# A macaron block with an SSM on one core: the gate's logits with the weights stationary in four column strips, transposed back by one instruction per group

## The reference

```python
def _L0_ffn_ref(hidden_states, gate_w, shared_gate, shared_up, shared_down, r_gate, r_up, r_down):
    ...
    shared_out = _swiglu(x, shared_gate, shared_up, shared_down)
    logits = x @ gate_w.T
    top_id = jnp.argmax(logits, axis=-1)
    score = jax.nn.sigmoid(jnp.max(logits, axis=-1))
    xs = x * score[:, None]
    ...
x = L0_attn_x
x = x + 0.5 * _L0_ffn_ref(_layernorm(x, axis=-1), ...)
x = x + _L0_attn_ref(_layernorm(x, axis=-1), ...)
x = x + 0.5 * _L0_ffn_ref(_layernorm(x, axis=-1), ...)
```

## Time and profile before

| | |
|---|---|
| median of 3 runs | 948.54 us (945.77 to 955.72) |
| the profiled execution | 946.78 us, its span 944.6 us |
| TensorE busy | 884.2 us, 94% of the span |
| TensorE weight load busy | 773.7 us, 82% |
| VectorE, ScalarE, GpSimd busy | 478.7, 383.5, 465.2 us |
| the logits matmuls, L434, TensorE busy | 33.5 us, 256 records |
| mean granted TensorE clock | 0.973 of full |

### The profile page before, as it was taken

The page is one execution under the profiler, slowest core; times in us unless marked ns, Lnnn a source line. Parts: engine busy times, 40 slices in busy tenths (PEclk is TensorE's granted clock), DMA queues, the critical chain, the costliest instruction groups (busy, mean ns, idle before and its releaser), DMA issues.

```text
span 944.6 us, 16359 instructions
## 1 busy us (share of the span) xinstructions
PE 884.2 (94%) x5422; PEld 773.7 (82%) x5423; DVE 478.7 (51%) x1008; ACT 383.5 (41%) x749; POOL 465.2 (49%) x427
## 2 busy tenths in 40 slices
PE   4999998999999999998999997999899999998998
PEld 3887787888878887887888997888788878887887
DVE  6657563333333334759898882765233323332453
ACT  3224222333333343445686763433233334333331
POOL 4424656033333305778999983576333242210883
PEclk9798999999999999998999997899999999999999
DMA  8594456246464315332011005548343555511567
GB/s 290 184 310 147 141 179 245 88 170 211 166 208 170 122 46 113 49 52 28 6 51 29 23 28 202 172 153 289 118 169 133 183 183 183 184 56 57 91 106 183
DMA packets 75292, 130.33 MB, mean 138 GB/s; under 512 B 6650, under 2 KB 67204, under 8 KB 70884
## 3 DMA queue, kind: packets, MB, share of 16 engines
q0 software_dynamic: 18688, 74.33, 25.9%
q1 hardware_dynamic: 56178, 55.21, 18.4%
q10 hardware_dynamic: 370, 0.02, 0.0%
HBM read 93.22 MB, written 36.32 MB: 137 GB/s over the span
## 4 chain that ended last, share of the span: by engine, by line
PE 73%; DMA 9%; POOL 6%; DVE 6%; issue 4%; ACT 1%; SPq 1%; ACTq 0%; POOLq 0%; DVEq 0%
PE bank L359 21%; PE bank L360 20%; PE bank L361 20%; DMA rows<-xs_sorted 8%; PE bank L426 3%; PE bank L434 3%; PE bank L559 3%; PE bank L528 2%; DVE v L1302 2%; POOL v L1535 2%; POOL hT_lo L1539 1%; POOL acc L1622 1%; DVE xT_lo L1031 1%; POOL rstd L1471 1%; POOL cbs L1497 1%
## 5 line engine op out<-in xcount | busy, mean ns | idle before, releaser
L359 PE MATMUL bank<-wr_hi,xT_hi 128*128 x312 | 130.8, 419 | 9.9 <-issue 7.6
L1596 POOL TENSOR_TENSOR wr_lo<-wr_raw,wr_hi 128x3072 fp32r<-128x3072 f32 x14 | 95.2, 6801 | 87.6 <-DMA wr_hi<-w_routed 87.6
L1622 POOL DMA_INDIRECT acc<-ys_sorted,pos x64 | 103.5, 1617 | 59.2 <-DMA ys_sorted<-rows 41.1
L361 PE MATMUL bank<-wr_lo,xT_hi 128*128 x312 | 123.9, 397 | 0.0
L360 PE MATMUL bank<-wr_hi,xT_lo 128*128 x312 | 123.9, 397 | 0.0
L1259 DVE TENSOR_TENSOR hf<-sg,bank 128x512 f32<-128x512 f32 x78 | 53.7, 689 | 136.2 <-PE bank L361 136.2
L1031 DVE TENSOR_TENSOR hT_lo<-bank,hT_hi 128x512 fp32r<-128x512 f32 x78 | 54.0, 692 | 125.3 <-ACT hT_hi L775 125.3
L359 PE MATMUL bank<-xT_hi,ws_hi 128*128 128x512 f32 x256 | 105.0, 410 | 3.9 <-DVE xT_lo L1031 3.1
L775 ACT ACTIVATE xT_hi<-bank 128x256 fp32r<-128x256 f32 (+1 forms) x126 | 56.4, 465 | 121.0 <-PE bank L528 95.7
L360 PE MATMUL bank<-xT_hi,ws_lo 128*128 128x512 f32 x256 | 103.0, 402 | 0.0
L361 PE MATMUL bank<-xT_lo,ws_hi 128*128 128x512 f32 x256 | 102.4, 400 | 0.0
(11 more groups left out here) (231 smaller groups left out, 2243.1 us busy)
## 6 DMA issues: line engine op xcount, KB each, us to landing
wr_raw<-w_routed POOLq DMA_DIRECT2D x16, 1536.0 KB, 7.1
wr_hi<-w_routed POOLq DMA_DIRECT2D x16, 1536.0 KB, 7.8
rows<-xs_sorted SPq DMA_DIRECT2D x78, 128.0 KB, 2.5
ys_sorted<-rows SPq DMA_DIRECT2D x78, 128.0 KB, 1.8
xn_kept<-xg SPq DMA_DIRECT2D x16, 512.0 KB, 3.2
rows<-xn_kept SPq DMA_DIRECT2D x16, 512.0 KB, 4.1
xg<-xn_kept SPq DMA_DIRECT2D x15, 512.0 KB, 5.0
acc<-x SPq DMA_DIRECT2D x8, 512.0 KB, 9.8
```

What stands on the lines that cost most here:

```text
L359: pe.matmul(o, a_hi, b_hi, start=start, stop=False, skip_group_check=True)
L361: return pe.matmul(o, a_hi, b_lo, start=False, stop=stop, skip_group_check=True)
L1596: pool.tensor_tensor(wr_lo[:, e % 2, :], wr_raw[:, :], f32(wr_hi[:, e % 2, :]), ALU.subtract).then_inc(s_wl, 1)
L1622: pool.indirect_dma_start(out=acc[:, tt, :], out_offset=None, in_=ys_dram, in_offset=bass.IndirectOffsetOnAxis(ap=pos[:, tt:tt + 1], axis= ...
```

## The change

The weights and the data change places. `gw_f` is padded with zeros from 8 to RG = 32 columns and is the stationary operand. The 4 tiles of a group go to 4 column strips of the array, 32 columns each, and stream 128 tokens; for each block of features the 4 strips follow each other. The result has tile t's experts on partitions 32t to 32t+7 and tokens along the free dimension. ScalarE copies this 128x128 block into `lgT` (two buffers), TensorE transposes it with one instruction (`logits_back`) into the next 128 columns of the same bank, and VectorE picks 8 of each 32 columns from there.

In the first stage the results go to other banks than the transpositions (`R1_LG`: bank 6 for groups 0 to 4, then 3, 5, 3), the transpositions no longer wait for VectorE's copy, and each transposition back stands after the next group's transpositions; the transpositions of group 6 stand before shared_down's second piece. In attention the transposition back of logits n-4 stands in iteration n between w_out and w_in.

```diff
+        R1_LG = (D2[0],) * (FB + 1) + (G2[1], U2[1], G2[1])
...
-            def logits(f, bank=LG, src=xTf):
+            def logits(f, bank=LG):
+
                 pe.wait_ge(s_xf, 2 * f + 2)
-                for t in range(GT):
-                    for kb in range(KB):
-                        mm = pe.matmul(bank[:, t * E:(t + 1) * E], src[:, kb, t * P:(t + 1) * P], gw_f[:, kb, :],
-                                       start=(t == 0 and kb == 0), stop=(kb == KB - 1), skip_group_check=True)
-                mm.then_inc(s_lg, 1)
+                for kb in range(KB):
+                    for t in range(GT):
+                        rs = slice(t * RG, (t + 1) * RG)
+                        mm = pe.matmul(bank[rs, 0:P], gw_f[:, kb, :], xTf[:, kb, t * P:(t + 1) * P], start=(kb == 0),
+                                       stop=(kb == KB - 1), skip_group_check=True, tile_position=(0, t * RG))
+                mm.then_inc(s_lq, 1)
+
+            def logits_back(f, bank=LG):
+                pe.wait_ge(s_lt, f + 1)
+                pe.transpose(bank[:, P:2 * P], lgT[:, f % 2, :], ident[:, :]).then_inc(s_lg, 1)
...
                         w_out_part(n - 2, 3)
+                    if live(n - 4):
+                        logits_back(f_ln3(n - 4))
                     if live(n):
                         w_in_part(n, 0)
...
             def r1_transposes(g):
-                if g > 0:
-                    pe.wait_ge(s_lgc, g)
                 transposes(g % 2, s_xn, g + 1, min(g, 1), f_r1(g))
...
             r1_transposes(1)
+            r1_back(0)
             pe.wait_ge(s_wsl, 1)
             shared_gu(0, 0, 0)
...
             r1_transposes(5)
+            r1_back(4)
             pe.wait_ge(s_wsl, 2)
             pe.wait_ge(s_setv, 12)
+            pe.wait_ge(s_lgc, FB + 1)
             shared_down(0, 0, 0)
             r1_logits(5)
+            r1_transposes(6)
+            r1_back(5)
             shared_down(0, 0, 1)
...
+            def logits_copy(f, bank=LG):
+                act.wait_ge(s_lq, f + 1)
+                if f >= 2:
+                    act.wait_ge(s_lg, f - 1)
+                act.activation(lgT[:, f % 2, :], bank[:, 0:P], ACT.Copy).then_inc(s_lt, 1)
...
                 for n in range(NG + 4):
                     if live(n - 1):
                         y_silu(n - 1, 2)
+                    if live(n - 4):
+                        logits_copy(f_ln3(n - 4))
                     if live(n):
                         first_tap(n, 0)
...
             def copy_logits(g, count, bank=LG):
                 dve.wait_ge(s_lg, count)
-                dve.tensor_copy(tiles(lg, g), bank[:, 0:GT * E].rearrange("p (t e) -> p t e", t=GT)).then_inc(s_lgc, 1)
+                dve.tensor_copy(tiles(lg, g), bank[:, P:2 * P].rearrange("p (t e) -> p t e", t=GT)[:, :, 0:E]).then_inc(s_lgc, 1)
```

More of the change, by code:

```diff
@@ L96, in build @@
         ones_r = sb("ones_r", [P, P], F32R)
-        gw_f = sb("gw_f", [P, KB, E], F32)
+        gw_f = sb("gw_f", [P, KB, RG], F32)
+        lgT = sb("lgT", [P, 2, P], F32)
         vec = sb("vec", [P, CB, 5], F32)
@@ L201, in build @@
         s_late = sem("small_loaded")
+        s_gwz = sem("gate_padding_cleared")
         s_x = [sem(f"x_loaded{g}") for g in range(NG)]
@@ L246, in build @@
         s_xf = sem("xTf_done")
+        s_lq = sem("logits_by_expert_done")
+        s_lt = sem("logits_by_expert_copied")
         s_lg = sem("logits_done")
@@ L719, in r1_logits, with r1_back @@
                 if g == 0:
-                    pe.wait_ge(s_xl, 2)
                     pe.wait_ge(s_late, 16 * 4)
-                logits(f_r1(g))
+                    pe.wait_ge(s_gwz, 1)
+                if 1 <= g < FB + 1:
+                    pe.wait_ge(s_lgc, g)
+                elif g == FB + 1:
+                    pe.wait_ge(s_sg, FB)
+                elif g == FB + 2:
+                    pe.wait_ge(s_h, FB)
+                elif g == FB + 3:
+                    pe.wait_ge(s_lgc, g - 1)
+                logits(f_r1(g), R1_LG[g])
+            def r1_back(g):
+                logits_back(f_r1(g), R1_LG[g])
             setup_ssm(0)
@@ L738, in _ @@
             r1_transposes(2)
+            r1_back(1)
             setup_ssm(7)
@@ L743, in _ @@
             r1_transposes(3)
+            r1_back(2)
             shared_gu(0, 0, 2)
@@ L747, in _ @@
             r1_transposes(4)
+            r1_back(3)
             shared_gu(0, 0, 3)
@@ L998, in _, with r1_copy @@
             act.activation(PQ[:, 0, :, :].rearrange("n a m -> n (a m)"), A2[:, :], ACT.Tanh).then_inc(s_seta, 1)
+            def r1_copy(g):
+                logits_copy(f_r1(g), R1_LG[g])
             xt_hi(0)
@@ L1003, in _ @@
             ws_high(1, slice(DN0, W))
+            r1_copy(0)
             xt_copy(t_r1(1))
             s_silu(0, 0, 0)
+            r1_copy(1)
             xt_copy(t_r1(2))
+            r1_copy(2)
             xt_copy(t_r1(3))
@@ L1009, in _ @@
             s_silu(0, 0, 1)
+            r1_copy(3)
             xt_copy(t_r1(4))
@@ L1013, in _ @@
             s_silu(0, 0, 3)
+            r1_copy(4)
             xt_copy(t_r1(5))
             s_hi(0, 0, 2)
+            r1_copy(5)
             xt_copy(t_r1(6))
             s_hi(0, 0, 3)
+            r1_copy(6)
             xt_copy(t_r1(7))
+            r1_copy(7)
             shared(0, 0)
@@ L1354, in _ @@
             dve.memset(GS[:, 0:1], 0.0)
+            dve.memset(gw_f[:, :, E:RG], 0.0).then_inc(s_gwz, 1)
             dve.memset(RS[:, :], 0.0)
@@ L1394, in r1_copy_logits @@
             def r1_copy_logits(g):
[L1395 removed]
+                copy_logits(g, g + 1, R1_LG[g])
             r1_stats(0)
```

10 lines of the change are left out of this document (5 added, 5 removed).

## The result

The changed kernel takes 967.88 us in the median (963.63 to 969.08), the kernel before 947.15 us beside it on the same chip (945.17 to 955.72). The ratio is 1.0195 with a 95% interval of 1.0135 to 1.0256: slower by 1.3 to 2.6%. The profiled execution took 963.63 us, its span is 961.8; the one of before took 946.78 with a span of 944.6.

A forecast was written before the change was run, and what follows sets the result against it. TensorE (PE) was taken as the bound, holding 73% of the chain. Attention's added waits, 4.5 + 2.6 + 1.6 + 0.6 + 3.0 = 12.3 us, less 0.5 in the first stage, gave +12 on 948.54: 960.5 us, range 953 to 968.

The forecast's parts named there:

- Both waits in attention: Attention: PE waits for ScalarE's lgT, then VectorE's late taps; +4.5 (n = 4, 5), +2.6, +1.6 and +0.6, +3.0 us.
- The clock: Rival: PE's new idle times bring one to three half-clock falls, up to 3 us each; 963.5 to 970.5 us; chance 0.15.
- The strips: Logits matmuls on PE: strips overlap two deep, about 0.95 us a group instead of 1.68, saving 0.75 at full clock.
- First stage: Before 72 us: PE done some 4 us earlier, mostly lost to a longer wait for the shared load; -0.5 us.
- near 71.5: First stage's end: the shared load still lands near 71.5 us, PE idling some 6 us before the first shared transpositions.
- that normalization comes out at the same time: First stage: group 6's normalization on VectorE, which the load's issue depends on, ends at the same time as before.
- the very sign that the prediction named as proof against itself: End of first stage: the shared stage starting 3 us earlier would show the forecast wrong.
- That ws_lo's subtraction would stand behind the copy of logits 0: First stage, VectorE: this subtraction, and the first gate matmuls with it, come after that copy; no separate size given.
- Strips in turn: Rival: column strips do not overlap, 1.7 us a group; waits stay, nothing saved; +18 or 966.5 us; chance 0.10.
- the waits are taken up by slack: Rival: unseen slack, mainly GpSimd's, absorbs most of the waits; -2 to +6, or 946.5 to 954.5 us; chance 0.12.
- All four at once: Rival: all four strips run together, 0.43 us a group; +8.5, or 957 us; chance 0.17.
- Faster if the copy is in time: Rival: lgT is there when w_out ends, so 16 groups save 1.1 us each; 938 us; chance 0.06.

The follow-up runs named there:

- e6: Changed kernel with idle matmuls added on PE to fill its two waits in n = 4 to 7; ratio 1.015 to the kernel before.
- e1: Changed kernel with ScalarE's copy of attention's logits moved early, to the end of the iteration before; ratio 0.998 to the kernel before.
- e2: Changed kernel with VectorE's logits copy in attention moved behind the taps of block 3; one run, 957.5 us beside 953.9 for the kernel before.
- e12: The probe: e10 plus six rows of added matmuls behind the first stage; 16 matmuls took 0.90 us on four strips, 3.41 on one.
- e10: Changed kernel with both ScalarE's copy early and VectorE's copy behind the taps, transposition back still after w_out; ratio 0.997 to the kernel before.
- e14: e11 with VectorE's ws_lo subtraction put back ahead of its copy of logits 0 in the first stage; ratio 0.983 to the kernel before.
- e11: e10 with GpSimd's first two routed-expert loads held until the first shared group's load has landed; ratio 0.989 to the kernel before.
- e9: Changed kernel with old logits form in attention and GpSimd's first two routed-expert loads held until the first shared load landed; ratio 0.997 to the kernel before.
- e5: Changed kernel with the two logits loops exchanged, each strip's four passes in a row; one run, 960.8 us beside 953.9 for the kernel before.
- e13: Kernel before with only GpSimd's first two routed-expert loads held until the first shared load landed; ratio 0.996 to the kernel before.

## Why the prediction was right, and where its steps were not

Forecast 960.5 us, range 953 to 968, slower; it came out as 967.88, or 20.7 over the 947.15 beside it where +12 was forecast. The direction and the mechanism are as worked out; the size is not. That the median lies inside the range, by 0.12 us, is luck: two of the four executions took more than 968.

**Both waits in attention: right.** L447 stands 1 to 3 us behind w_out and waits for `lgT`, VectorE's copies wait for PE, w_in part 1 for `v`, b_out at n = 8 for `acc`. At n = 6 the forecast was 1.95 us for the first wait and 1.80 was measured. Put into PE's own frame (transposition to transposition, the changed kernel less before), the iterations lost 4.8 and 3.2 (n = 4, 5), 3.9 (n = 6), 2.0 (n = 7) and 1.2 + 3.6 (n = 8 and the next), and the end gave 0.7 back. The forecast had 4.5 together, 2.6, 2.2, 3.0 and 0: 12.3 against 18.3. With the clock held up from n = 4 to 7 (e6) the same frames lost 3.7 + 0.9, 2.7 and 2.8, of which 0.8 are the fillers'. That is the forecast's 4.5, 2.6 and 2.2 nearly to the tenth.

**The clock: a term left out of the sum.** The prediction had it as a rival with 0.15. The falls at n = 4 and 5 cost 4.6 us (e6). The one behind b_out costs some 1.4, an estimate from its rows: ten steps of w_out at 0.213 us and a group of 0.99, where 0.119 and 0.58 are the rows at full clock. These 6.0 us are the whole of what was missing, so the waits by themselves were sized right, and the rival's "one to three falls" came on top of them, at 2.3 us for each of the long ones where the rival had up to 3. The row that should have weighed more was the earlier trace rows: PE idle for 2.77 us, then 0.50. The changed kernel's first wait at n = 4 was to be nearly as long. What the two waits do together can be read from e1, e2 and the 0.5 us rows above. In e1 the second wait of n = 4 to 7 alone brought no fall. In e2 the first alone brought falls of 3.4 us, at n = 4 and 6. With both, the fall again begins behind the first wait and before the second, and lasts 6.8 us; the second seems to lengthen it.

**The strips: near in size, wrong reason.** The forecast was 0.95 us a group, because two passes of one matmul would block the others. Measured is 0.58 to the next row and 0.75 with both changes of mode. The Trainium skill's page "TensorE: Matmul & The Clock Gate", Part 3, has all tiles run together in one span, which makes 0.43 us with the rows' 0.107 (an estimate). The Trainium skill's page "TensorEngine Tiling (Array Packing)", Key Properties, has a switch of mode drain the engine. The probe agrees with both: four strips side by side at 0.107 a pass on each, and 0.15 us a change. The prediction had the two side by side and took a third value between its bounds, where their sum, one span and two changes, is what the group takes. The saving is 1.68 - 0.75 - 0.12 (the transposition back) = 0.8 us an iteration, and the iterations of 18.88 and 18.80 us, which take 17.97 and 17.99 in e10, show about that (0.9 and 0.8); the forecast had 0.75 to 0.8.

**First stage: the right bottleneck, mis-sized.** PE was done 9.5 us earlier instead of 4. Two reasons stand in the rows, though no run prices them apart: a group takes 0.58 instead of 0.95, and the granted clock, which fell to 0.50 three times among the old logits, stayed at 1.00 until PE idled. The load did swallow most, but it did not land "near 71.5": it was issued 4.3 us earlier (56.06). Group 6's normalization ended on VectorE at 51.6 instead of 55.9, which the step "that normalization comes out at the same time" denied. Group 6's transpositions, which the load had waited for (until 60.2), were done at 52.7, and the store of group 6 let the load go. The shared stage started 3.5 us earlier, the very sign that the prediction named as proof against itself. PE then idled 8.46 us and not some 6. Of the 3.5, 0.9 were left where attention begins, less than executions scatter. That ws_lo's subtraction would stand behind the copy of logits 0 and hold the first gate matmuls was right (e14).

**The rivals.** "Strips in turn" is out (0.58, not 1.7), "the waits are taken up by slack" is out for both together; for each alone it is half true, since e1 and e2 lose only 4.3 and 6.8 us against the kernel before. "All four at once" and "the clock falls" both happened, with the forecast's waits. "Faster if the copy is in time" was the right condition but too high a price: e10 has it in time and gains 3.3 us in attention, not 8 times 1.1. In e10 PE's wait at n = 5 (0.88 at 514.23) is for GpSimd's `hT_lo`, so there the logits save nothing, and two mode changes cost 0.3 a group.

**What stays open.** The ratios of e11 and e9 differ by twice what the stretch does. The clock's falls do not follow the length of the waits: in the changed kernel there is one behind the 1.80 of n = 5 and none behind the 1.80 of n = 6, in e2 it is the other way round, and in e5 none follows the 2.77 of n = 4. How passes of different strips overlap in e5 is not shown either.

## What to carry to other kernels

When a result has to cross engines more often than before (here PE, ScalarE, PE, VectorE instead of PE, VectorE), the price is not the added instructions, 0.3 us each, but the places in the queues where they stand: put each hand-over right behind its producer and ahead of nothing that someone else waits for. The same new matmuls gave a kernel 2% slower with the copies where they were, and with two of them moved one that is 0.3% faster (interval up to no change). And where the trace of before shows the granted clock falling behind a wait as long as the one that a change brings, its price belongs in the sum, not among the rivals: here it was 6 of 18.3 us. It is a price with a chance, since the same wait brought the fall in one execution and not in another.

## What the runs showed of the hardware that was not expected

- Fp32 matmuls with 32 stationary columns on four column strips run four at once, both passes of each: 0.028 us a pass against 0.107 on one strip (e12). Each change between strips and the whole array costs 0.15 us. For a group of 8 matmuls that is 0.43 + 0.3, so the changes eat a quarter of what the strips would save (0.3 of 1.25).
- The granted clock can fall although PE is recorded as busy without a gap. In the probe this happened over the 8-column matmuls of row (6), from 1.00 to 0.50 (2.4 to 1.2 GHz). The stretches of the probe (same columns as above):

```profile
66.00:68.00 2.00, 2.00 (x27) 2.00 (x19) 0.00 (x0) 0.00 (x0) 0.00 (x0) 1.00 0.94 320
...
78.00:79.00 1.00, 1.00 (x12) 1.00 (x11) 0.00 (x0) 0.00 (x0) 0.00 (x0) 1.00 0.00 0
79.00:80.00 1.00, 1.00 (x11) 1.00 (x10) 0.00 (x0) 0.00 (x0) 0.00 (x0) 0.95 0.00 0
80.00:82.00 2.00, 2.00 (x11) 2.00 (x11) 0.00 (x0) 0.00 (x0) 0.00 (x0) 0.50 0.03 8
```

  The fall stands 2.5 us behind the start of row (6), so the probe alone does not rule out row (5), with its changes of mode, as the cause. In the first stage of the kernel before and of e13 the clock falls three times (at 30.5, 40.7 and 64.6 us). Each fall comes within 1.2 us of the end of a group of old logits, and PE has no wait over 0.3 us there. In the kernels with strips in the first stage it stays up until PE idles, but for e14. There it falls at 30.0 us, behind waits of 0.96 and 0.76 and the small matmuls of the power recursion, which also stand in front of the first two falls of the kernel before. So the old form is a likely cause and not a shown one, and not every group of it brings a fall.
- A load of 512 KB took 12.3 us beside two of 1536 KB issued just before it, and 4.3 us when these were held back (e11).
- Added idle matmuls made attention's stretch 3.8 us shorter, with the clock held up (e6). One fall of 6.8 us cost 2.3 us (e5 against the changed kernel).
